# Where TensorE's waits stand before a burst of scores: two stack waits a slot earlier, and the wait for the maximum written last

## The reference, cut to what matters

```
x = LN(x + self_attention(x))              # 16 heads of 8, biases on q, k, v
x = LN(x + cross_attention(ctx, x, ctx))   # q from x; k and v from ctx
x = LN(x + qlinear(gelu(qlinear(x, W1, b1)), W2, b2))   # FFN with 8-bit quantised operands

attention(q, k, v): softmax(q @ k.T / sqrt(8)) @ v, per head, then an output projection
qlinear: scale and zero point from the minimum and maximum of the whole activation
```

## Time and profile before

| | us |
|---|---|
| median of 3 executions | 356.62 |
| lowest, highest | 354.52, 357.43 |
| the profiled execution | 355.31 |
| its span, first to last instruction | 353.5 |
| mean granted clock of TensorE, of full speed | 0.916 |

### The profile page before, as it was taken

How to read it: one execution, slowest core, us unless ns; L and a number is a source line. 1 busy time by engine, 2 the same in 40 slices (tenths; PEclk the granted TensorE clock), 3 DMA queues, 4 the chain that set the end, 5 groups by cost and what they waited for, 6 DMA issues and landing times.

```text
span 353.5 us, 13237 instructions
## 1 busy us (share of the span) xinstructions
PE 265.0 (75%) x4897; PEld 171.0 (48%) x4899; DVE 314.0 (89%) x720; ACT 252.5 (71%) x502; POOL 187.0 (53%) x382
## 2 busy tenths in 40 slices
PE   3678887989989999999899988898883365102980
PEld 2446564656656666666665655555551122001660
DVE  5756799989999999999999999999889599997894
ACT  2135877988889888888888887887762599605855
POOL 6234869656675666657675667665222006400275
PEclk9999999999999999999999999999995578755797
DMA  1352323233332332323323242332000000000034
GB/s 52 89 159 69 99 80 88 63 108 90 97 107 74 107 104 84 101 84 102 106 83 107 79 124 84 96 94 71 5 3 0 0 0 0 0 0 3 1 90 149
DMA packets 48998, 25.19 MB, mean 71 GB/s; under 512 B 6440, under 2 KB 48808, under 8 KB 48936
## 3 DMA queue, kind: packets, MB, share of 16 engines
q1 hardware_dynamic: 46936, 23.76, 23.4%
q10 hardware_dynamic: 2000, 0.59, 0.7%
HBM read 9.39 MB, written 2.10 MB: 32 GB/s over the span
## 4 chain that ended last, share of the span: by engine, by line
DVE 32%; PE 30%; POOL 14%; issue 13%; DMA 4%; ACT 3%; SPq 2%; ACTq 0%; POOLq 0%; DVEq 0%; another core or an unknown queue 0%
DVE neg_max L850 14%; PE ps L1083 8%; PE ps L1109 7%; DVE h_ext L957 5%; DVE h_ext L958 5%; DMA arena_h<-parts_sk 4%; POOL rstd L531 3%; PE ps L1167 2%; PE ps L1156 2%; SPq L399 2%; PE ps L1124 2%; PE ps L1144 2%; PE ps L1131 2%; PE ps L1251 1%; POOL o_root L598 1%
## 5 line engine op out<-in xcount | busy, mean ns | idle before, releaser
L850 DVE TENSOR_REDUCE neg_max<-ps 128x8 f32<-128x1024 f32 x128 | 157.2, 1228 | 18.5 <-PE ps L1083 16.0
L652 ACT ACTIVATE probs<-ps 128x1024 f32<-128x1024 f32 x64 | 65.6, 1025 | 19.7 <-PE ps L1090 18.2
L1083 PE MATMUL ps<-arena_h 31*128 31x128 f16 x1024 | 52.8, 221 | 27.3 <-DVE neg_max L850 17.9
L663 ACT ACTIVATE probs<-ps 128x1024 f32<-128x1024 f32 x64 | 65.7, 1026 | 8.5 <-PE ps L1090 8.5
L1083 PEld LDWEIGHTS ps<-arena_h 31*128 31x128 f16 x1024 | 31.0, 94 | 59.9 <-DVE neg_max L850 35.6
L1090 PE MATMUL ps<-arena_h 32*128 32x128 f16 x1024 | 51.7, 219 | 0.6 <-ACT probs L652 0.5
L528 POOL TENSOR_TENSOR var_eps<-mean_var,eps_col 128x1 f32<-128x1 f32 x64 | 12.2, 191 | 73.4 <-DVE mean_var L833 73.4
L1109 PE MATMUL ps<-probs,arena_q 128*32 128x128 f32 x1024 | 42.1, 283 | 0.9 <-issue 0.9
L1109 PE MATMUL ps<-probs,arena_h 128*32 128x128 f32 x1024 | 41.6, 281 | 0.2 <-ACT probs L652 0.2
L531 POOL TENSOR_TENSOR rstd<-var_eps,minus_half 128x1 f32<-128x1 f32 x64 | 35.2, 550 | 5.0
L1090 PEld LDWEIGHTS ps<-arena_h 32*128 32x128 f16 x1024 | 29.6, 93 | 1.6 <-ACT probs L663 0.5
(11 more groups left out here) (155 smaller groups left out, 626.4 us busy)
## 6 DMA issues: line engine op xcount, KB each, us to landing
arena_h<-parts_sq SPq DMA_DIRECT2D x48, 64.0 KB, 2.0
arena_h<-parts_ck SPq DMA_DIRECT2D x48, 64.0 KB, 2.1
arena_h<-parts_cq SPq DMA_DIRECT2D x48, 64.0 KB, 2.0
arena_h<-parts_sk SPq DMA_DIRECT2D x45, 64.0 KB, 2.0
xT_in<-in_xT_dram SPq DMA_DIRECT2D x16, 128.0 KB, 2.6
xN_in<-in_xN_dram SPq DMA_DIRECT2D x16, 128.0 KB, 2.7
cT_in<-in_cT_dram SPq DMA_DIRECT2D x16, 128.0 KB, 2.4
cN_in<-in_cN_dram SPq DMA_DIRECT2D x16, 128.0 KB, 2.6
```

The lines of the kernel that those rows point to most:

```text
L652: act.activation(probs[1][:, :], ps_s2, ACT.Exp, scale=SCALE).then_inc(ex, 1)
L663: act.activation(probs[0][:, :], ps_s2, ACT.Exp, scale=SCALE).then_inc(ex, 1)
L850: dve.tensor_reduce(neg_max[b.par][:, HH * half:HH * half + HH], ps_s1.rearrange("p (h k) -> p h k", h=HH), AXX, ALU.max, negate=True).the ...
L1083: ins = pe.matmul(ps_s1[:, at:at + S], q[r:r + MAX_AT, j, :], kk[r:r + MAX_AT, j, :], start=True, stop=True, skip_group_check=True)
```

## The change

Two things are moved in PE's program; nothing else is touched. In `scores(half)` the order of the waits becomes (`s_maxrow`), `ex`, `mx`; it was (stacks), `mx`, (`s_maxrow`), `ex`. The two waits for the stacks go to a new function `stacks()`, which waits for the stacks of `task(k + 3)`, the b of the next slot, and is called between the output projection (L1191) and the turning of the attention output (L1199).

```diff
                     s, s_half = (z, 1) if half == 0 else (a, 0)
-                    if b is not None:
-                        if half == 0 and b.half == 0:
-                            for n in (b.q, b.k):
-                                pe.wait_ge(s_stack[n][b.ring], landed(b.pair, RING, 16 * NTERM))
-                        need(pe, mx, 2 * b.pos + half)
                     if s is not None:
                         if s_half == 0:
                             pe.wait_ge(s_maxrow[s.par], 16 * (s.pos // 2 + 1))
                         need(pe, ex, 2 * s.pos + s_half)
+                    if b is not None:
+                        need(pe, mx, 2 * b.pos + half)
...
+                def stacks():
+
+                    t = task(k + 3)
+                    if t is not None and t.half == 0:
+                        for n in (t.q, t.k):
+                            pe.wait_ge(s_stack[n][t.ring], landed(t.pair, RING, 16 * NTERM))
...
                     pe.matmul(ps_o[:, 0:D], attT[:, :], (wo_self if x.kind == "S" else wo_cross)[:, :],
                               start=True, stop=True, skip_group_check=True).then_inc(oo, 1)
+                stacks()
                 if w is not None:
 
                     pe.wait_ge(an, w.pos + 1)
```

## The result

| us | changed | before | ratio |
|---|---|---|---|
| median of 6 and 6 executions | 360.42 (359.17 to 363.33) | 355.10 (354.52 to 357.43) | 1.0162 [1.0119, 1.0204] |
| the profiled execution, its span | 360.47, 358.7 | 355.31, 353.5 | |
| the same kernel a second time, on another set of runs | 360.07 | 354.55 | 1.0160 [1.0123, 1.0196] |

What follows compares the result with a forecast made beforehand. The closed ring of maximum and score burst on one buffer was taken as the bound. Order 2.0, early bursts 0.3 and late stacks 1.5 sum to 3.8 us, on 356.62 giving 360.4; range 355.8 to 363.5.

Steps and rivals of the forecast that it cites:

- The ring as the bound: Attention, 59.6 to 254 us: maximum and score burst alternate on one `ps_s1` buffer; time between maxima is paid in full.
- Which wait the load carries: Before each score burst: the wait written first is carried by PE's weight load, the others run as separate instructions before it.
- the rival by which the maximum would have stayed on the load: Score bursts: the last written wait is on the load; ring some 3 us shorter, 355.1 with late stacks; chance 0.10.
- The prices: Maximum's end to load 0.115 us, load to next maximum 0.475, in every burst; two slots take 7.26.
- Sum for the order: Writing `mx` last in the score bursts: 2.0 us from 59.58 us to the end, plus 0.3 before.
- Before the ring is steady: Bursts before 59.6 us, about half stalled by other work: 0.3 us slower, ends 0 and 0.9.
- The stack waits a slot earlier: Stack waits after the output projection: late landings hold PE's turnings and the burst behind them; 1.5 us slower, ends 0 and 3.
- My upper bound, 3: High end, in us, of the late-stack cost, if as many landings again are late.
- ScalarE behind L1204: ScalarE's copies of attT and cq_full wait behind PE's delayed turnings; forecast to add nothing.
- The median: Base of the sum: 356.62 us for the kernel before, 1.31 above its profiled execution.
- The range: Whole kernel's forecast time: 355.8 us, for the maximum staying on the load, to 363.5.
- the first rival: Score bursts: the maximum's wait stays on the weight load; 353.6 us, with late stacks 355.1; chance 0.10.

Runs made afterwards that it cites:

- e4: The changed kernel with `mx` moved one separate PE wait instruction further ahead of the load in all bursts; 369.03 us, 1.0428 to the kernel before.
- e3: The kernel before with `mx` written first and the stack waits behind it, in the same burst; 351.56 us, 0.9915 to the kernel before.
- e1: The kernel before with only the order changed: `mx` written last, stack waits still in the burst; 357.33 us, 1.0099 to the kernel before.
- e2: The kernel before with only the stack waits moved a slot earlier, `mx` written first; 354.39 us, 0.9989 to the kernel before.
- e5_shift_30: The changed kernel with 60 waits met at once, 30 more instructions, ahead of PE's first instruction; 1.0125 to the kernel before.
- e9: The changed kernel with the stack waits one step later, between the turnings of attention output and x1; 359.76 us, 1.0123 to the kernel before.
- e5_shift_73: The changed kernel with 73 more PE instructions, waits met at once, at the start and in three early slots; 1.0186 to the kernel before.
- e8: The changed kernel with the stack waits one step earlier, ahead of the output projection L1191; 1.0247 to the kernel before.

## Why the prediction was right, point by point

- **The ring as the bound:** right. 0.107 us per burst more (e4) comes back as 9.4 us.
- **Which wait the load carries:** right. The wait written first is on the load, the others on separate instructions ahead of it, as read from three places of the earlier trace rows. e3 and e1 differ in nothing but this, and the rival by which the maximum would have stayed on the load is excluded.
- **The prices:** 0.115 and 0.475 in every burst, to 1 ns of what was taken from the tail of the attention. 7.26 for two slots, as forecast: the maxima at 233.66 and 240.92 of the changed kernel, for the stretch of the earlier trace rows, are 7.26 apart.
- **Sum for the order:** 2.3 forecast, 3.5 measured in e1 (2.3 to 4.7). The steady ring gave what was computed: from the maximum of burst 23 to that of burst 127, the changed kernel takes 192.02 us and the one before 187.98, and 2.0 of these 4.0 us are left when the stalls are taken off (3.2 against 1.2).
- **Before the ring is steady:** the 0.3 us is the term that was most undersized. The maximum of burst 23 starts at 67.05 us in the changed kernel (67.52 in its second profile) and at 65.33 in the kernel before: 1.7 (2.2) more. In the two profiles of the change 1.3 and 1.2 of it is what the fallen clock costs behind the stall at burst 20, of which the prediction says nothing. From burst 127 on to the end the changed kernel is 0.6 shorter, so that 1.7 + 4.0 - 0.6 makes the 5.2 between the profiled executions. The fall to 0.50 near 60 us stands in five of the eight profiles with the stack waits ahead of the burst (the change twice, e2, e5_shift_30, e9; not e4, e5_shift_73, e8), and in none of the five that have them in the burst. The length of the idle time doesn't decide it alone: e8 idled 2.57 us without it, e5_shift_30 fell after 1.42. With one profile of most kernels, how often it comes, and what part of the 0.6% to 0.7% is due to it, stays open.
- **The stack waits a slot earlier:** the mechanism was right, with the stall at L1204 and a landing-to-burst time of 0.32 and 0.41 for my 0.37 and 0.48. The 1.5 us was mis-sized too. In the profiled pair late stacks from burst 24 on cost 2.1 us more; all that the place of the waits costs measured 0.6% to 0.7%, 2.2 to 2.6 us, give or take 2, with the clock's part in it. I had counted the late bursts of one profile as if they were properties of those bursts. They are draws: about one stack in four lands late (7 of 28 took over 2.8 us in each of the two first profiles), and moving a wait earlier makes more of the draws count. My upper bound, 3, lies above what was measured.
- **ScalarE behind L1204:** forecast to add nothing; its copy waited 2.2 us in four stalls behind L1204 and 4.6 in four behind L1213, but burst-to-maximum times stayed at 0.45 in the stalled bursts and the gaps of the bursts behind them at 0.115, from burst 44 on. Not on the path there.
- **The median:** the sum was hung on a median of three that stood 1.5 us high. This error and the undersized terms cancelled.
- **The range:** its lower end, 355.8, is said to stand for the first rival, whose own sum is 355.1; the range doesn't hold it. Nothing hung on it.

## What to carry to other kernels

The place of a wait in the code isn't the place where it is run. Where several waits stand before one instruction, look in the trace which one the instruction itself carries (here the one written first) and give that place to the wait that comes last on the critical path; here one line moved up is worth 0.7% over the tuned kernel. A wait for a DMA belongs directly before what needs the data: each step ahead puts what stands between on the path whenever the transfer is late, and a transfer with slack on average can still be late one time in four. And a stall isn't over when it ends: look at the granted clock behind it.

## What was not expected of the hardware

- A wait on a separate PE instruction costs 0.062 us more than on the weight load, the second such instruction 0.107 more; and the burst behind takes 0.024 longer until its last scores are there (0.475 against 0.451). That this is because it isn't queued yet was not shown.
- Instruction fetch of TensorE, one 16 KB packet of 0.9 to 1.7 us every 256 instructions or so, goes with 64 KB transfers inside SBUF of as much as 4.0 us in place of 1.9, when it begins soon after their issue.
- After an idle time of PE of 1.4 to 2.3 us TensorE's granted clock fell to 0.50 for 3.4 us in some profiles (five of thirteen) and not in others; in the changed kernel that cost 1.3 us.
- The profile's name for what ended a wait is the semaphore nearest to the instruction, so reordering waits renames the bound: "DVE neg_max" fell from 114 to 53 entries while it remained what all waited for.
